# Gathering the rows of the smaller-numbered expert beside the last expert's tiles, in the second feed-forward of a macaron layer

## The reference

```
def ffn(x):                                   # x: 2048 tokens x 512
    y = swiglu(x, sw1, sw2, sw3)              # shared expert, hidden width 704
    scores = softmax(x @ gate_w)              # 8 experts
    weights, indices = top_k(scores, 2)       # each token goes to two experts
    for e in range(8):                        # hidden width 352
        y = y + cw[:, e:e+1] * swiglu(x, rw1[e], rw2[e], rw3[e])
    return y
x = x + 0.5 * ffn(layernorm(x))
x = x + attention(layernorm(x))
x = x + 0.5 * ffn(layernorm(x))
```

## Time and profile before

| | us |
|---|---|
| median of three runs | 1736.2 |
| the three runs | 1732.48, 1736.2, 1738.26 |
| profiled execution, whole | 1725.97 |
| its span (first to last instruction) | 1724.2 |
| PE busy in the span | 1633.2 (95%) |
| DVE, POOL, ACT busy | 1017.4, 974.0, 837.7 |

### The profile page before, as it was taken

One profiled execution on the slowest core, in us unless ns is written; L12 is line 12 of the kernel. 1 busy time (PEld: TensorE's weight loads), 2 busy tenths in 40 slices (PEclk: granted clock), 3 DMA queues, 4 the chain that ended last, 5 costly groups with the idle time before them and its releaser, 6 DMA issues.

```text
span 1724.2 us, 24273 instructions
## 1 busy us (share of the span) xinstructions
PE 1633.2 (95%) x8164; PEld 1287.5 (75%) x8164; DVE 1017.4 (59%) x1738; ACT 837.7 (49%) x1172; POOL 974.0 (56%) x736
## 2 busy tenths in 40 slices
PE   6999999999988889999999999999999999999997
PEld 5778889998867666666666666556777889999985
DVE  5554322222477579999999999985655422222226
ACT  4422223233223238999999999893442223233220
POOL 3106575317557658788878888860232547731645
PEclk9999999999988979999999999999999999999998
DMA  9306544334462220100010000004101535533427
GB/s 339 111 17 237 198 166 151 135 104 151 130 192 63 73 57 20 38 19 20 19 38 19 20 19 20 7 20 149 55 1 56 199 147 179 189 126 122 142 83 247
DMA packets 67843, 175.69 MB, mean 102 GB/s; under 512 B 10768, under 2 KB 11664, under 8 KB 65424
## 3 DMA queue, kind: packets, MB, share of 16 engines
q1 hardware_dynamic: 54896, 100.48, 18.1%
q0 software_dynamic: 12832, 73.67, 12.0%
HBM read 102.29 MB, written 55.84 MB: 92 GB/s over the span
## 4 chain that ended last, share of the span: by engine, by line
PE 56%; DVE 24%; DMA 7%; issue 6%; ACT 5%; SPq 2%; POOL 1%; DVEq 0%; ACTq 0%; POOLq 0%
PE PS L1145 10%; PE PS L1147 9%; PE PS L1146 9%; DVE nmf_later L1944 6%; DVE Pl L1971 4%; DVE nmf_first L1944 3%; DMA xn<-x_routed 3%; DVE Ph L1963 3%; DMA xs<-x_routed 2%; PE PS L1282 2%; PE PS L1287 2%; PE PS L1285 2%; PE PS L1284 2%; PE PS L1286 2%; PE PS L1283 2%
## 5 line engine op out<-in xcount | busy, mean ns | idle before, releaser
L2120 POOL TENSOR_TENSOR Pl<-PT,Ph 128x1024 fp32r<-128x1024 f32 x162 | 420.1, 2610 | 105.1 <-ACT Ph L1645 73.2
L1636 ACT ACTIVATE PT<-PS 128x1024 f32<-128x1024 f32 x256 | 259.1, 1015 | 28.5 <-PE PS L1376 27.4
L1645 ACT ACTIVATE Ph<-PT 128x1024 fp32r<-128x1024 f32 x198 | 208.9, 1055 | 3.6
L1396 PE MATMUL PS<-Ph,V 128*65 128x512 f32 x496 | 200.0, 403 | 1.6 <-ACT OT L1653 1.6
L1944 DVE TENSOR_REDUCE nmf_later<-PS 128x1 f32<-128x1024 f32 x160 | 188.9, 1211 | 12.6 <-PE PS L1358 12.5
L1398 PE MATMUL PS<-Pl,V 128*65 128x512 f32 x496 | 195.7, 394 | 0.0
L2020 POOL TENSOR_TENSOR W<-raw,W 128x544 fp32r<-128x544 f32 x144 | 190.1, 1355 | 1.5
L1376 PE MATMUL PS<-QS,KS 98*128 98x512 f32 x512 | 175.9, 427 | 12.7 <-DVE nmf_later L1944 8.8
L1911 DVE TENSOR_TENSOR thid<-thid,PS 128x352 f32<-128x352 f32 x78 | 40.6, 521 | 245.7 <-ACT thid L1570 245.7
L1358 PE MATMUL PS<-KS,QS 96*128 96x512 f32 x512 | 166.8, 409 | 8.3 <-DMA KS<-early_lo 3.3
L1570 ACT ACTIVATE thid<-PS 128x352 f32<-128x352 f32 x78 | 36.3, 465 | 260.8 <-PE PS L1287 260.8
(11 more groups left out here) (197 smaller groups left out, 3973.4 us busy)
## 6 DMA issues: line engine op xcount, KB each, us to landing
raw<-ffn_w POOLq DMA_DIRECT2D x18, 2176.0 KB, 10.3
y_routed<-ytile SPq DMA_DIRECT2D x78, 256.0 KB, 2.2
xn<-x_routed SPq DMA_DIRECT2D x40, 256.0 KB, 3.4
x_routed<-xq SPq DMA_DIRECT2D x1, 9984.0 KB, 29.4
xs<-x_routed SPq DMA_DIRECT2D x38, 256.0 KB, 3.3
QS<-later_hi SPq DMA_DIRECT2D x112, 64.0 KB, 2.0
raw<-ffn_w SPq DMA_DIRECT2D x6, 768.0 KB, 10.5
raw<-ffn_w SPq DMA_DIRECT2D x16, 272.0 KB, 4.1
```

The costliest lines, as they stand in the source:

```text
L1396: e.matmul(PS[0:VCOL, ob, :], V[:, b * QT + kt, g, :], high_part(u)[:, js], start=kt == 0, stop=False)
L1636: e.activation(PT[:, u % PTBUF, :], PS[:, i:i + 2, :].rearrange("p b n -> p (b n)"), ACT.Exp, scale=SCALE).then_inc(p_ready.sem, 1)
L1645: e.activation(high_part(u)[:], PT[:, u % PTBUF, :], ACT.Copy).then_inc(ph_act.sem, 1)
L2120: e.tensor_tensor(low_part(u)[:], PT[:, u % PTBUF, :], high_part(u)[:], ALU.subtract).then_inc(pl_pool.sem, 1)
```

## The change

In the second feed-forward, the row of the expert of the smaller number is gathered by itself: right behind the split of unit 9, POOL waits until the writes of all tiles ahead of expert 7's first one have landed (a count that it works out in a register), and issues 16 gathers into a new tensor `first_rows`, with a place for each token tile. After the last tile only the other 16 gathers remain. They too have a place for each tile, in the memory of `early_pairs` and `late_pairs`: eight come right away, eight behind the wait for down(2), with no wait for a combine. Two gathers share a semaphore count, so a combine waits for the gathers of two tiles, and for all 16 first rows. The last five combines are moved up in the order of the work, so that all 16 stand ahead of down(5). The first feed-forward keeps its order.

```
+        if s:
+            work.extend(("first_rows", item[2]) for slot in later for item in slot)
...
-                        work.extend(gathers[:PAIRS])
-                        del gathers[:PAIRS]
+                        now = NT if s else PAIRS
+                        work.extend(gathers[:now])
+                        del gathers[:now]
...
+    sums = [slot for g in (LATE, *FIRST) for slot in combined(1, g)]
+    work.extend(item for slot in ffn(1, sums[:11] + [sums[11] + sums[12], sums[13] + sums[14], sums[15]])
+                for item in slot)
...
+    first_rows, at = place("first_rows", (P, NT, D), F32, g_at[2])
...
+                rows = [last_rows(t), first_rows[:, row_place[t], :]]
+                dve.wait_ge(first_rows_in, combines[-1][1])
+                dve.wait_ge(*two_in(t))
...
+            elif kind == "first_rows":
+                t, = key
+                if row_place[t] == 0:
+                    for i in range(2):
+                        e.reg_alu(ahead, base[E - 2], 1 - i, ALU.add)
+                        e.reg_alu(ahead, ahead, 1, ALU.logical_shift_right)
+                        e.reg_alu(ahead, ahead, 4, ALU.logical_shift_left)
+                        out_ = e.snap(ahead, min_val=16, max_val=16 * ((TILES + 1) // 2))
+                        e.wait_ge(tile_out[i].sem, out_ + (tile_out[i].at[1, i] - 16))
+                        e.sem_inc(tiles_ahead.sem, 1)
+                        pool.wait_ge(tiles_ahead, i)
+                e.indirect_dma_start(first_rows[:, row_place[t], :], None, y_routed,
+                                     bass.IndirectOffsetOnAxis(ap=pos[:, 1, t:t + 1], axis=0),
+                                     bounds_check=ROWS_OUT - 1, oob_is_err=False).then_inc(first_rows_in.sem, 16)
+            elif kind == "gather" and key[0] == 1:
+                _, t = key
+                for i in (TILES - 2, TILES - 1):
+                    pool.wait_ge(tile_out[i % 2], 1, i)
+                if row_place[t] >= 2 * PAIRS:
+                    pool.wait_ge(down_done, 1, step_of(LATE, 2), LATE * TPG + TPG - 1)
+                e.indirect_dma_start(last_rows(t), None, y_routed,
+                                     bass.IndirectOffsetOnAxis(ap=pos[:, 0, t:t + 1], axis=0),
+                                     bounds_check=ROWS_OUT - 1, oob_is_err=False).then_inc(two_in(t)[0].sem, 16)
```

More of the change, by code:

```diff
@@ L498, in order_of_work @@
     work.extend(("shared_in", 1, i) for i in range(3, len(SHARED_PIECES)))
-    work.extend(item for slot in ffn(1, [slot for g in (LATE, *FIRST) for slot in combined(1, g)]) for item in slot)
+    sums = [slot for g in (LATE, *FIRST) for slot in combined(1, g)]
+    work.extend(item for slot in ffn(1, sums[:11] + [sums[11] + sums[12], sums[13] + sums[14], sums[15]])
+                for item in slot)
     work.append(("end",))
@@ L593, in macaron @@
     pairs = [early_pairs[:, i] for i in range(PAIRS)] + [late_pairs[:, i] for i in range(PAIRS)]
+    first_rows, at = place("first_rows", (P, NT, D), F32, g_at[2])
+    assert at <= arena and unit_slot(E - 1) > 0 and LATE_SLOT > 0
     qtok, at = place("qtok", (P, NT, D), F32, arena)
@@ L670, in macaron @@
     gathered = [signal(f"gathered{i}", 32) for i in range(2 * PAIRS)]
+    tiles_ahead, first_rows_in = signal("tiles_ahead"), signal("first_rows_in", 16)
     wqkv_in = [signal(f"wqkv_in{c}", 16) for c in range(DC)]
@@ L717, in macaron, with last_rows, two_in @@
                     for i, key in enumerate(of for of in combines if of[0] == s)}
+    row_place = {key[1]: i for i, key in enumerate(of for of in combines if of[0] == 1)}
+    def last_rows(t):
+        return pairs[row_place[t] // 2][:, row_place[t] % 2, :]
+    def two_in(t):
+        of = [u for u in row_place if row_place[u] == row_place[t] | 1]
+        return gathered[row_place[t] // 2], 1, of[0]
     def pair_before(s, t):
@@ L828, in macaron @@
         elif kind == "gather":
-            gathered[pair_of_tile[tuple(key)]].plan(*key)
+            s, t = key
+            if s == 0:
+                gathered[pair_of_tile[s, t]].plan(s, t)
+            elif row_place[t] % 2:
+                gathered[row_place[t] // 2].plan(s, t)
+        elif kind == "first_rows":
+            if row_place[key[0]] == 0:
+                for i in range(2):
+                    tiles_ahead.plan(i)
+            first_rows_in.plan(*key)
         elif kind == "combine":
@@ L1829, in combine @@
         def combine(s, t):
-            pair = pairs[pair_of_tile[s, t]]
-            dve.wait_ge(gathered[pair_of_tile[s, t]], s, t)
+            if s == 0:
+                pair = pairs[pair_of_tile[s, t]]
+                rows = [pair[:, 0, :], pair[:, 1, :]]
+                dve.wait_ge(gathered[pair_of_tile[s, t]], s, t)
+            else:
+                rows = [last_rows(t), first_rows[:, row_place[t], :]]
+                dve.wait_ge(first_rows_in, combines[-1][1])
+                dve.wait_ge(*two_in(t))
             if s == 0 or t // TPG != LATE:
                 dve.wait_ge(shared_added, s, t)
-            e.scalar_tensor_tensor(X[:, t, :], pair[:, 0, :], pair_w[:, 0, t:t + 1], X[:, t, :],
+            e.scalar_tensor_tensor(X[:, t, :], rows[0], pair_w[:, 0, t:t + 1], X[:, t, :],
                                    ALU.mult, ALU.add).then_inc(half_summed.sem, 1)
             dve.wait_ge(half_summed, s, t)
-            e.scalar_tensor_tensor(X[:, t, :], pair[:, 1, :], pair_w[:, 1, t:t + 1], X[:, t, :],
+            e.scalar_tensor_tensor(X[:, t, :], rows[1], pair_w[:, 1, t:t + 1], X[:, t, :],
                                    ALU.mult, ALU.add).then_inc(combined.sem, 1)
@@ L1989, in gpsimd_program @@
         base = [e.alloc_register(f"base{i}") for i in range(1, E)]
+        ahead = e.alloc_register("ahead")
         def unit_load(s, u):
```

## The result

The changed kernel takes 1745.6 us in the median of seven runs (1741.8 to 1747.2), the kernel before 1736.2 us beside it (seven runs, 1732.5 to 1738.3). The ratio is 1.0052, 95% interval 1.0033 to 1.0071. The forecast was 1732.8 with a range of 1729.4 to 1738.2; the time lies outside it, and on the other side of the kernel before. The profiled execution of the changed kernel has a span of 1744.5 us, 20.3 us more than that of the kernel before.

The account below looks back on a forecast made before the run. The tail was taken as a chain: down(2), gather, landing, then DVE's work with PE between. Down(2) and landing 0.7, combines and fewer waits 3.1, outputs -0.4: 3.4 us, median 1736.2 to 1732.8, range 1729.4 to 1738.2.

Parts of the forecast that it names:

- The 22 us of idle POOL that hide them: POOL's idle time between unit 9's split and the last tile's landing hides sixteen gathers of 20.8 to 22.2 us.
- tiles that slow down beside the gathers: Sign that the prediction is wrong: the tiles' rows on PE stand further apart than before beside the early gathers.
- Rival 3: Last tile's write lands behind the gathers, POOL starts at 1677.1, tile loads stop PE: 6.5 us slower, 1742.7; chance 0.05.
- The median, 10.2 us above the profiled execution before, from 1736.2 to 1732.8: Whole kernel: the profiled execution goes from 1726.0 to 1722.6, and the median keeps its 10.2 us distance above it.
- The write behind the tiles: Last tile's write beside the gathers lands in 3.3 us instead of 2.0, so POOL's next gather starts 1.3 us later, 1670.2.
- Each us beyond 1670.2 lost on PE: First gather behind the tiles: nothing is lost up to a POOL start of 1670.2, then PE loses one for one.
- C1 directly behind C0: First combines behind the tiles: C1 already has its row and waits for nothing; g1 at 1678.15 against 1678.16.
- C8, g4 and g5: Second block on DVE: combine C8 starts at 1699.1, gate g4 at 1703.5, gate g5 at 1711.4.
- These 9.5 us of waiting are worth almost nothing: DVE's waits for rows in the first block go away, but PE runs without stops there; it gains 0.2 us.
- Down(5) to the last sum's start 3.7 us, at the half clock: End of the program: price kept from before, so the last sum starts at 1717.2 and ends at 1717.9.
- the outputs: Five tiles written in the last 3 us instead of two: 0 to 1 us more until the last lands, 0.4 taken.
- The two rules of the Trainium skill: Landing estimated at 2.6 us, making the sum 4.9; last write at most twice its time. Rows (3.6; 10.17 us load) preferred.

Follow-up runs that it names:

- `a_fourth`: The changed kernel, unedited, in a later group of runs where the kernel before takes 1723.2 us; 1720.2 us, ratio 0.9986.
- `h_half`: Against the changed kernel, moves the gathers of the first rows of C0 to C7 behind the tiles, two tiles sharing a semaphore; 1725.2 us, ratio 1.0010 to before.

## Why the prediction was wrong, step by step

The step that failed is the price of the sixteen early gathers for the engines beside them. The forecast put it at nothing; in the second kind of group, to which the timed runs belong, it is 12.8 us (34.9 us of the table above against 22.1). What holds the signals up there is not known further than the experiments show. A second and smaller miss is the term from down(5) to the last sum.

`a_fourth` is of the same kind as the profile on which the forecast was built. Its unit 9 split ends at 1630.77 + 10.56 = 1641.33, 5.49 us ahead of the earlier trace rows, so I add 5.49 us to its times:

| | before | forecast | `a_fourth` + 5.49 |
|---|---|---|---|
| first early gather | - | 1647 | 1646.96 |
| last one done | - | 1668.6 | 1667.60 |
| POOL's first gather behind the tiles | 1668.95 | 1670.2 | 1670.95 |
| C0 | 1673.91 | 1675.2 | 1675.95 |
| g1 | 1678.16 | 1678.15 | 1678.85 |
| late gathers | 1693.93 | 1693.7 | 1694.45 |
| C8 | 1699.77 | 1699.1 | 1699.38 |
| g4 | 1706.56 | 1703.5 | 1703.74 |
| g5 | 1712.34 | 1711.4 | 1711.64 |
| last sum starts | 1718.14 | 1717.2 | 1719.66 |
| end of the span | 1724.2 | 1720.8 | 1722.8 |

**"The 22 us of idle POOL that hide them": wrong, and it decides the result.** The room was there and the sixteen gathers fit into it. But their cost was taken from POOL's own time alone. In the second kind of group ACT waits beside them for signals up to 12 us late, and PE with it; the changed kernel loses 12.8 us, and the kernel without the gathers nothing. The prediction named the sign, tiles that slow down beside the gathers, and it came true. Rival 3 gave 1742.7, close to the measured time, by another mechanism: the last tile's write late behind the gathers. That agreement is chance. POOL's gather started 2.8 us after that write was issued, as before; it was the tile that came late.

**"The median, 10.2 us above the profiled execution before, from 1736.2 to 1732.8": right in size, wrong in what was taken to follow.** The gap is there after the change as well, 10.1 us, and it lies in the first scatters. But it meant that the timed runs were of another kind than the profile. The sum of the prediction was read from a profile in which rows of indirect transfers cost PE nothing, and applied to runs in which one of them did. A loss beside the new row could not be forecast for certain from the loss beside the first scatters: the second feed-forward's scatters have late signals too, and PE was idle for 0 to 1.2 us of 55 there. The three runs of before and the profile's own time, side by side in the table, were the one sign of it ahead of the result.

**The write behind the tiles: right in kind, short by 0.7 us.** It was given 1.3 us more than before. The last write of `a_fourth` is issued at 1660.6 (the writes of `y_routed` in its last 30 us of tiles: count, duration, first and last start), and POOL's gather starts 4.9 us later, where the earlier trace rows have 2.85. That is 2.0 us more.

```profile
L1102 SPq DMA_DIRECT2D y_routed<-ytile x5: 319/320/320, 1635.7 to 1660.6; - x5
```

**Each us beyond 1670.2 lost on PE: right.** POOL at 1670.95 gave g1 0.7 us late and down(2) with it.

**C1 directly behind C0; C8, g4 and g5: right**, the last three within 0.3 us of the forecast. For C8 this is two misses that cancel: the late gathers start 0.75 us later than forecast, so that down(2) brings no gain, and landing to use takes 3.6 us where 4.1 were taken.

**"These 9.5 us of waiting are worth almost nothing": not settled.** `h_half`, with the moved combines and without the early rows of C0 to C7, is 5.0 us slower than `a_fourth`, and PE waits for gates in it. This suggests that a part of the change is worth more than the sum has because the other part makes it needed. But `h_half` also has longer waits of its own, and no run has the early rows with the combines where they stood.

**"Down(5) to the last sum's start 3.7 us, at the half clock": the mis-sized term.** In the earlier trace rows down(5) is 0.50 us a product, which is the full clock: from 1714 to 1718 the granted clock was 0.93. After the change the wait ahead of down(5) is 4.9 us. The timeline of PE, then the stretches of before and of `a_fourth`:

```profile
1708.27 0.79 PE L1259 MATMUL PS<-W,hidh 128*128 128x512 f32 x1 [4.88 <-DVE hidh L1852]
```

```profile
1714.00:1718.00 4.00, 3.71 (x9) 1.48 (x8) 3.79 (x6) 0.00 (x0) 1.28 (x1) 0.93 0.85 278
```

```profile
1708.00:1715.00 7.00, 5.86 (x8) 2.29 (x8) 4.49 (x7) 0.00 (x0) 0.00 (x0) 0.50 0.40 150
```

PE is at 1.2 GHz for all of down(5), the sums come 1.45 us apart, and the way from down(5) to the last sum's start takes 5.9 us instead of 3.7. The text foresaw the idle time and the half clock, and then took the price of a stretch that had run at the full one. Against before's profile `a_fourth` gains 1.4 us instead of 3.4 (by the interval of the runs, 0.7 to 4.1). The 2.0 us that are missing are 2.2 of this term and 0.2 by which g5 comes late, less 0.5 from the outputs: 2.4 us behind the last sum, where 2.9 were expected.

**The two rules of the Trainium skill.** By the Trainium skill, DMA: Bandwidth & Descriptors, "Anatomy of one DMA — SWDGE (gpsimd) path", an estimate of 2.6 us for the landing, C8 would have followed two gathers sooner than it did; it took 1693.89 - 1690.26 = 3.6 us, as the earlier trace rows have it for C0, and the measurement decides. By the Trainium skill, same page, "Queues, rings and completion order", the last write could take at most twice its own time. In `a_fourth` it took 4.0 us beside the gathers, twice its 2.0, and did not fall behind them. The row of 10.17 us gave a rival that no run bears out.

## What to carry to other kernels

Idle time of the queue that issues transfers is not free room: cost a row of them by what happens to the signals of the engines beside it, and look for such a row elsewhere in the program, where the same loss may already stand. A late signal costs only where the next engine has nothing else to do; the last tiles were such a place, the second scatters hardly. When the profiled execution and the timed runs of one kernel differ by more than the runs among themselves, find out where before forecasting from the profile, since it may show another condition than the one that is timed. Put the unedited changed kernel into every group of experiments, and take the price of a step from a row at the clock that the step will have.

## What the hardware did that was not expected

- ACT waited up to 13.7 us in the last tiles, 3.2 in undisturbed ones, for signals of PE that were due, while POOL issued indirect gathers 1.3 us apart. The longest of these waits ended 2.1 to 2.5 us after the last gather, with 64 bytes a token as with 2 KB (waits of 11.6 and 9.6 us).
- Such waits stood in three groups of runs (before at 1733.9 to 1737.6), always beside indirect transfers of POOL or up to 3.2 us behind them, and in none of four groups (1723.2 to 1724.0), with every kernel of a group alike in the stretch from 150 to 172 us.
- Plain copies from the same queue, 256 KB each, were issued 0.53 us apart (16 in 8.46 us) against 1.30 for gathers. At 302 GB/s beside the tiles they cost PE nothing: 7.00 us busy of 7.
